# Keys of the second stage run one block further ahead of values

## The chip, the cores and the metric

The kernel runs on one core of a Trainium2 chip. The metric is the device time of one execution in microseconds (us), lower is better. A core has TensorE (PE, matmuls; its weight loads are listed as PEld), VectorE (DVE), ScalarE (ACT), GpSimd (POOL) and SyncE (SP, which here only starts DMAs). They run their own instruction lists in order and meet at semaphores.

## The reference, cut to what matters

```python
# layer 0: group norm, q/k/v, softmax attention over 4096 positions, output projection, residual
x = _L0_conv_ref(x, ...)
# layer 1
t = _to_tokens(x)                                   # (4, 4096, 128)
kv = silu(_ln_t(t) @ W_kv)                          # 8 heads x 128 keys and 8 x 128 values
s = einsum('hd,bthd->bth', q_proj, k)               # one score per head and token
m = cummax(s); e = exp(s - m); u = cumsum(e)
w = cumsum(e[..., None] * v); t = t + (w / u).mean(heads)
# top 2 of 8 experts by a softmax router, over the normed tokens
t = t + _L1_ffn_ref(_ln_t(t), router_w, router_b, expert_w, expert_b)
```

## The kernel before, in words

The first stage (layer 0) takes the first two thirds of the span and is not touched. The second stage (`scan_attention_and_experts`) does layer 1 for 32 blocks of 512 tokens: block i is chunk s = i // 4 of batch element i % 4. Four blocks with the same s are called a super here.

One loop over steps j = 0 to 43, with eight slots h in each, is written out on every engine. In slot h of step j an engine does its part for head h of the **values** of block j - 5 (V_LAG), for head h of the **keys** of block j, and for the **experts** of block j - 11 (F_LAG) or j - 12. So steps 0 to 4 have keys alone, 5 to 10 keys and values, 11 to 31 all three, 32 to 36 values and experts, the rest experts alone.

- Keys of a block: POOL makes xf (`scaled`, L1110) and xl (`low`, L1116), ACT rounds xh (`high`, L1333), PE runs three matmuls a head (`key`, L1242), ACT the silu (L1337), PE the scores of four heads at a time (`row_sums`, L1258). After the fourth block of a super its scores are complete, and VectorE turns them into weights in the next step (`rows_at`): running maximum and difference in slot 0 (L1441, L1447), after an exp on ACT in slot 2 (L1394, between two activation table loads) the running sum and a reciprocal in slot 3 (L1452, L1458), a product in slot 4 (L1462). SP writes these rows to DRAM (`weight_rows`, four DMAs) and reads them back spread over 128 partitions, half a block (1 MB) at a time (`weight_spread`, tile bq).
- The token norm of the super after the next also hangs on the key steps (`norm1_at`): ACT squares four blocks in slots 4 and 5, PE means in slot 6 and slot 0 of the next step, VectorE the variance (slot 1), ACT `norm_scale` in slot 7 of that step: Ln and Exp (L1326, L1328).
- Values of a head: PE three matmuls into one of three PSUM banks (`value`), which wait until the scan of head h - 3 is done; ACT silu (L1341) and one minus the weight (L1347); VectorE product (`weigh`, L1469) and scan along the tokens (`scan`, L1477). POOL adds the heads (L1131 to L1138), VectorE adds the residual (L1484).
- Experts: POOL gates four pairs (L1124, 1024 columns each), PE runs eight f32 matmuls (L1278), VectorE adds the result (`output`, L1496) at the start of slot 4. The router (`norm2_at`) works in steps j with j % 4 = 1 (logits on PE, `gate_scale` on ACT in slot 7: L1368, L1370) and 2 (choice of two experts on VectorE, slots 0 to 4). Where j % 4 = 1, `norm_scale` and `gate_scale` of the two norms stand between one pair of table loads (L1412, L1417).

The two norms and the router share one PSUM bank, st_ps.

By j % 4 the extra work before is: 0, rows and first half of the token norm; 1, its second half, logits, both scales, and the first use of the new weights; 2, choice of experts; 3, nothing. These are called here the steps of rows, of logits, of choice, and plain.

## Time and profile before

| | |
|---|---|
| time, median of 3 runs (lowest, highest) | 2654.93 us (2654.89, 2656.35) |
| the profiled execution: its own time | 2654.88 us |
| the profiled execution: span of the core | 2653.2 us |
| busy: PE, DVE, POOL, ACT | 95%, 83%, 77%, 70% |
| first value silu of step 5 | 1879.6 us |
| step 36, the last with values, begins | 2569.47 us |
| TensorE clock granted, mean | 0.99 |

Start times are microseconds from the beginning of the span. A step is read here from VectorE's product for head 0 (L1469) to the next step's. Busy times overlap between engines; an engine that is less busy than the stretch is long waited in it, and the profile names what ended its wait.

### The profile page before, as it was taken

What the parts mean: (1) busy time and instruction counts of PE and PEld (TensorE: products, weight loads), DVE (VectorE), ACT (ScalarE), POOL (GpSimd) and SP (SyncE); (2) the same over time, 40 slices, a digit from 0 to 9 for tenths busy, and PEclk for the clock granted to TensorE, in tenths of its full rate; (3) what the DMA queues carried; (4) which work ended last, traced back from release to release, by engine and by line L of the source; (5) the groups of instructions that cost most, each with busy time, mean ns of one, the idle gap of its engine ahead of it and who ended that gap; (6) DMA issues with size and microseconds to landing.
All of it is one profiled execution on the core that took longest, in us unless ns stands there. A gap on an engine that the chain in (4) does not pass through costs nothing.

```text
span 2653.2 us, 36314 instructions
## 1 busy us (share of the span) xinstructions
PE 2526.4 (95%) x10665; PEld 1836.3 (69%) x10665; DVE 2190.9 (83%) x3276; ACT 1855.0 (70%) x3414; POOL 2032.4 (77%) x1492
## 2 busy tenths in 40 slices
PE   6999999999999999999999999998889999999878
PEld 4788877788887778888778878875445555555443
DVE  6788887788888778888788888873699889988995
ACT  5677777677777767677776667776887777777650
POOL 5787877778887777887678877886458989888883
PEclk9999999999999999999999999999989999999999
DMA  1000000010000010000000100101435666565555
GB/s 68 5 13 9 9 13 9 10 43 9 9 17 9 9 41 9 13 13 9 9 9 9 37 13 9 40 21 49 155 134 214 227 228 237 185 257 209 208 211 215
DMA packets 58102, 198.35 MB, mean 75 GB/s; under 512 B 12752, under 2 KB 15376, under 8 KB 40496
## 3 DMA queue, kind: packets, MB, share of 16 engines
q1 hardware_dynamic: 57904, 196.03, 21.0%
q8 instruction: 85, 1.39, 0.2%
q14 instruction: 113, 0.93, 0.1%
HBM read 178.04 MB, written 17.96 MB: 74 GB/s over the span
## 4 chain that ended last, share of the span: by engine, by line
PE 46%; POOL 26%; issue 14%; DVE 7%; ACT 4%; DMA 2%; SPq 0%; POOLq 0%; DVEq 0%; ACTq 0%
POOL p_lo L222 23%; PE m_ps L360 5%; PE om_ps L389 5%; PE s_ps L375 5%; PE om_ps L391 5%; PE om_ps L390 5%; PE s_ps L377 5%; PE s_ps L376 5%; PE mo_ps L1278 3%; DVE v_ps L1469 2%; DVE ay L1477 2%; PE k_ps L1234 1%; PE row_ps L1258 1%; PE v_ps L1234 1%; DMA bq<-weight_rows 1%
## 5 line engine op out<-in xcount | busy, mean ns | idle before, releaser
L222 POOL TENSOR_TENSOR p_lo<-pf,p_hi 128x512 fp32r<-128x512 f32 x1024 | 1319.5, 1293 | 390.7 <-ACT p_hi L512 388.0
L507 ACT ACTIVATE pf<-s_ps 128x512 f32<-128x512 f32 x1024 | 613.2, 599 | 508.1 <-PE s_ps L377 506.8
L651 DVE TENSOR_REDUCE mx<-m_ps 128x1 f32<-128x512 f32 x1024 | 701.4, 686 | 255.1 <-PE m_ps L360 248.3
L667 DVE TENSOR_TENSOR sum_ps<-sum_ps,pf 128x512 f32<-128x512 f32 x960 | 662.1, 690 | 20.0 <-ACT pf L507 19.6
L512 ACT CAST p_hi<-pf 128x512 fp32r<-128x512 f32 x1024 | 627.3, 613 | 0.0
L375 PE MATMUL s_ps<-q_hi,kd_hi 128*128 128x512 f32 x1024 | 424.6, 415 | 0.0
L360 PE MATMUL m_ps<-w_both,q_hi 128*128 128x512 f32 x1024 | 404.8, 397 | 7.7 <-DVE mx L651 6.5
L389 PE MATMUL om_ps<-p_hi,v_hi 128*128 128x512 f32 x1024 | 401.8, 392 | 6.1 <-POOL p_lo L222 6.1
L377 PE MATMUL s_ps<-q_lo,kd_hi 128*128 128x512 f32 x1024 | 399.7, 390 | 0.0
L376 PE MATMUL s_ps<-q_hi,kd_lo 128*128 128x512 f32 x1024 | 399.7, 390 | 0.0
L390 PE MATMUL om_ps<-p_hi,v_lo 128*128 128x512 f32 x1024 | 399.1, 390 | 0.0
L391 PE MATMUL om_ps<-p_lo,v_hi 128*128 128x512 f32 x1024 | 398.9, 390 | 0.0
L1477 DVE TENSOR_TENSOR_SCAN ay<-ay,carry,v_ps 128x512 f32<-128x512 f32 x224 | 286.8, 1280 | 8.5
L1124 POOL TENSOR_TENSOR xg<-gate_b,tv 128x1024 f32<-128x1024 f32 x108 | 258.6, 2398 | 9.3 <-DMA gate_b<-gate_rows 3.6
L1278 PE MATMUL mo_ps<-xg,ew 128*128 128x512 f32 x464 | 234.9, 605 | 10.6 <-POOL xg L1124 9.3
L1341 ACT ACTIVATE v_ps<-v_ps 128x512 f32<-128x512 f32 x256 | 150.3, 587 | 131.1 <-PE v_ps L1236 129.4
L360 PEld LDWEIGHTS m_ps<-w_both,q_hi 128*128 128x128 f32 x1024 | 192.9, 188 | 62.6 <-DVE mx L651 19.5
L389 PEld LDWEIGHTS om_ps<-p_hi,v_hi 128*128 128x128 f32 x1024 | 192.1, 188 | 58.1 <-POOL p_lo L222 16.4
L375 PEld LDWEIGHTS s_ps<-q_hi,kd_hi 128*128 128x128 f32 x1024 | 192.6, 188 | 51.8 <-issue 15.1
L376 PEld LDWEIGHTS s_ps<-q_hi,kd_lo 128*128 128x128 f32 x1024 | 192.6, 188 | 49.9 <-issue 12.7
L377 PEld LDWEIGHTS s_ps<-q_lo,kd_hi 128*128 128x128 f32 x1024 | 192.3, 188 | 41.6
L391 PEld LDWEIGHTS om_ps<-p_lo,v_hi 128*128 128x128 f32 x1024 | 192.2, 188 | 40.5
(226 smaller groups left out, 3587.5 us busy)
## 6 DMA issues: line engine op xcount, KB each, us to landing
bq<-weight_rows SPq DMA_DIRECT2D x64, 1024.0 KB, 6.7
gate_b<-gate_rows SPq DMA_DIRECT2D x60, 1024.0 KB, 5.0
xb<-in_x_dram SPq DMA_DIRECT2D x8, 1024.0 KB, 6.1
rb_sb<-inverse_rows SPq DMA_DIRECT2D x32, 256.0 KB, 3.7
tokens<-xb SPq DMA_DIRECT2D x32, 256.0 KB, 2.0
tp<-tokens SPq DMA_DIRECT2D x32, 256.0 KB, 5.4
rb<-norm_rows SPq DMA_DIRECT2D x32, 256.0 KB, 5.5
tv<-tokens SPq DMA_DIRECT2D x32, 256.0 KB, 6.5
```

The lines of the kernel that those rows point to most:

```text
L222: nc.gpsimd.tensor_tensor(p_lo[:, r, :], pf[:, r, :], p_hi[:, r, :].bitcast(F32), ALU.subtract).then_inc(lo_done, 1)
L360: pe.matmul(m_ps[:, j % 2, :], q_hi[:, n % QRING, sub * C:(sub + 1) * C], kp[:, chunk * BANK:(chunk + 1) * BANK], start=True, stop=True).t ...
L375: pe.matmul(dst, kd_hi[:, ks], q_hi[:, q, :], start=False, stop=False, skip_group_check=True)
L376: pe.matmul(dst, kd_lo[:, ks], q_hi[:, q, :], start=False, stop=False, skip_group_check=True)
L377: pe.matmul(dst, kd_hi[:, ks], q_lo[:, q, :], start=False, stop=True, skip_group_check=True).then_inc(s_pe, 1)
L389: pe.matmul(o, v_hi[:, t, :], p_hi[:, r, :], start=(t == 0), stop=False)
L390: pe.matmul(o, v_lo[:, t, :], p_hi[:, r, :], start=False, stop=False)
L391: pe.matmul(o, v_hi[:, t, :], p_lo[:, r, :], start=False, stop=(t == KT - 1)).then_inc(pv_pe, 1)
L507: nc.scalar.activation(pf[:, g % RING, :], s_ps[:, g % 2, :], ACT.Exp, scale=SCALE).then_inc(exp_done, 1)
L512: nc.scalar.copy(p_hi[:, g % RING, :], pf[:, g % RING, :]).then_inc(hi_done, 1)
L651: nc.vector.tensor_reduce(mx[:, n % 2, sub, chunk:chunk + 1], m_ps[:, j % 2, :], AX.X, ALU.max).then_inc(m_max, 1)
L667: nc.vector.tensor_tensor(sum_ps[:], sum_ps[:], p, ALU.add).then_inc(sum_done, 1)
```

## The change

Keys no longer go with the step number alone. `key_slots(j, h)` gives the keys (block and head) that belong to slot h of step j: one head as a rule, two in the slots that AHEAD lists. In steps 5 to 8 that is slot 3, in steps 9 and 10 slots 2 and 5: eight heads, so one block. From step 11 on keys are those of block j + 1, and step 31 has none. Everything that hangs on the key steps moves with them, rows and token norm too; values, router and experts stay. `begun(j)` gives the blocks whose head 0 falls into step j, for SP's queue. The ring of xh and xl has eight places instead of seven. `norm_scale` gets its own pair of table loads. Room is made in SBUF: ebf and qcol lie in acc, rst2 in var2, place1 and place2 are one tile, zeros is one column that the scans read 512 times. `mean` waits for the gates of the super four back.

```diff
-    NP, NV, NX = 8, 9, 7
+    NP, NV, NX = 8, 9, 8
+    AHEAD = {V_LAG: (3,), V_LAG + 1: (3,), V_LAG + 2: (3,), V_LAG + 3: (3,), V_LAG + 4: (2, 5), V_LAG + 5: (2, 5)}
...
-        zeros = sb("zeros", [C, TOK])
+        zeros = sb("zeros", [C, 1])
...
+        def key_slots(j, h):
+            n = HEADS * j + h + sum(len(at) for step, at in AHEAD.items() if step < j) + sum(at < h for at in AHEAD.get(j, ()))
+            return [divmod(n + i, HEADS) for i in range(2 if h in AHEAD.get(j, ()) else 1)]
+
+        def begun(j):
+            return [k for h in range(HEADS) for k, e in key_slots(j, h) if e == 0]
...
+                for k in begun(j):
+                    if stage(k + NP):
+                        load_p(k + NP)
+                    if k % B == 2 and k // B + 1 < SUPERS:
+                        norm_rows(k // B + 1)
+                    if stage(k + 2) and k:
+                        spread(sp, k + 2)
...
-                if rows_at(j) is not None:
-                    weight_rows(rows_at(j))
+                for k in begun(j):
+                    if rows_at(k) is not None:
+                        weight_rows(rows_at(k))
...
             def mean(s):
+                after(pe, gt_act, s - 3)
...
-                    if stage(k):
-                        silu_key(k, h)
-                    if rows_at(j) is not None and h == 2:
+                    for k, e in key_slots(j, h):
+                        if stage(k):
+                            silu_key(k, e)
+                        if rows_at(k) is not None and e == 2:
...
+                        if norm1_at(k, 1) is not None and e == 7:
+                            nc.scalar.preload_act_table_set("natural_log_exp_and_others")
+                            norm_scale(norm1_at(k, 1))
+                            nc.scalar.preload_act_table_set("silu_and_others")
...
-                    if h == 7 and (norm1_at(j, 1) is not None or norm2_at(j, 1) is not None):
+                    if h == 7 and norm2_at(j, 1) is not None:
                         if norm2_at(j, 1) != SUPERS - 1:
                             nc.scalar.preload_act_table_set("natural_log_exp_and_others")
-                        if norm1_at(j, 1) is not None:
-                            norm_scale(norm1_at(j, 1))
-                        if norm2_at(j, 1) is not None:
-                            gate_scale(norm2_at(j, 1))
+                        gate_scale(norm2_at(j, 1))
                         nc.scalar.preload_act_table_set("silu_and_others")
...
-                    if rows_at(j) is not None:
-                        s = rows_at(j)
-                        if h == 0:
-                            maxima(s)
-                            shifted(s)
+                    for k, e in key_slots(j, h):
+                        if rows_at(k) is not None:
+                            s = rows_at(k)
+                            if e == 0:
+                                maxima(s)
+                                shifted(s)
```

POOL's `scaled` and `low`, PE's `key`, `row_sums`, `square_mean` and `mean`, ACT's `high`, squares and VectorE's `sums`, `inverse`, `new_weights` and `variance` are put under `key_slots` in the same way.

## Rows read from the trace of the kernel before

**Rows 1.** The page: busy time of the engines.
```profile
PE 2526.4 (95%) x10665; PEld 1836.3 (69%) x10665; DVE 2190.9 (83%) x3276; ACT 1855.0 (70%) x3414; POOL 2032.4 (77%) x1492
```

**Rows 2.** Engines by stretch: steps 20, 21, 22, 23 (rows, logits, choice, plain).
```profile
core 0: us, PE busy (x) PEld busy (x) DVE busy (x) ACT busy (x) POOL busy (x), PEclk, DMA share, GB/s
2205.16:2233.45 28.29, 26.47 (x112) 14.72 (x109) 25.38 (x24) 19.57 (x34) 25.74 (x15) 1.00 0.41 147
2233.45:2257.40 23.95, 23.95 (x107) 14.07 (x106) 19.45 (x22) 21.00 (x38) 21.40 (x13) 1.00 0.90 334
2257.40:2279.70 22.30, 20.54 (x80) 11.38 (x79) 21.50 (x39) 16.42 (x31) 17.47 (x12) 1.00 0.51 173
2279.70:2298.55 18.85, 18.85 (x78) 11.38 (x76) 17.89 (x20) 13.06 (x24) 18.85 (x12) 1.00 0.74 274
```

**Rows 3.** VectorE's waits, 1879 to 2590 us: total us, times, longest.
```profile
DVE v_ps L1469 <- DMA bq<-weight_rows: 17.1, 8, 6.8
```

**Rows 4.** Timeline of VectorE, steps 20 to 22: its waits, and slot 4's scan.
```profile
2215.79 0.70 DVE L1469 TENSOR_TENSOR v_ps<-bq,v_ps 128x512 f32<-128x512 f32 x1 [0.81 <-ACT v_ps L1341]
...
2224.11 1.28 DVE L1477 TENSOR_TENSOR_SCAN ay<-ay,carry,v_ps 128x512 f32<-128x512 f32 x1
...
2233.45 0.70 DVE L1469 TENSOR_TENSOR v_ps<-bq,v_ps 128x512 f32<-128x512 f32 x1 [1.75 <-DMA bq<-weight_rows]
...
2257.40 0.70 DVE L1469 TENSOR_TENSOR v_ps<-bq,v_ps 128x512 f32<-128x512 f32 x1 [4.07 <-ACT v_ps L1341]
```

**Rows 5.** Timeline of ScalarE at the end of step 21, slot 7.
```profile
2251.67 0.59 ACT L1337 ACTIVATE sk<-k_ps 128x512 f32<-128x512 f32 x1
2252.28 1.28 ACT L1412 ACT_TABLE_LOAD   x1
2253.57 0.72 ACT L1326 ACTIVATE v_r<-v_r,epsc 128x512 f32<-128x512 f32 x1
2254.33 0.63 ACT L1328 ACTIVATE v_r<-v_r 128x512 f32<-128x512 f32 x1
...
2256.72 0.58 ACT L1341 ACTIVATE v_ps<-v_ps 128x512 f32<-128x512 f32 x1
```

**Rows 6.** The chain of waits, step 23: pieces on TensorE (start, length).
```profile
2276.02 0.50 PE v_ps L1234
...
2276.97 1.00 PE row_ps L1258 x8
...
2281.11 0.86 PE mo_ps L1278 x2
...
2282.20 0.23 PE v_ps L1235
...
2297.13 0.23 PE v_ps L1234
```

**Rows 7.** Engines by stretch: steps 5, 9 and 11.
```profile
1884.55:1903.27 18.72, 14.79 (x64) 8.70 (x64) 15.89 (x18) 17.72 (x30) 8.45 (x6) 1.00 0.64 248
...
1957.71:1979.00 21.29, 18.08 (x91) 10.52 (x89) 17.23 (x21) 20.81 (x38) 13.63 (x11) 1.00 0.62 236
...
2000.70:2018.24 17.54, 15.45 (x67) 9.12 (x66) 17.26 (x18) 13.23 (x24) 14.83 (x10) 1.00 0.76 263
```

**Rows 8.** Timeline of VectorE, steps 8 to 10: weights done, and its waits.
```profile
1950.32 0.67 DVE L1462 TENSOR_TENSOR b_r<-b_r,e_r 128x512 f32<-128x512 f32 x1
...
1957.71 0.70 DVE L1469 TENSOR_TENSOR v_ps<-bq,v_ps 128x512 f32<-128x512 f32 x1 [1.18 <-DMA bq<-weight_rows]
```

**Rows 9.** The chain of waits, step 8: the DMAs of the weights.
```profile
1952.02 1.47 DMA weight_rows<-b_r
1953.50 4.19 DMA bq<-weight_rows
```

**Rows 10.** Engines by stretch: steps 31 (plain) and 32 (rows).
```profile
2465.30:2484.16 18.86, 18.86 (x78) 11.40 (x76) 17.91 (x19) 12.54 (x23) 18.51 (x11) 1.00 0.80 284
2484.16:2510.88 26.72, 20.22 (x57) 10.99 (x54) 24.94 (x24) 12.58 (x20) 20.31 (x12) 0.81 0.30 105
```

More of the change, by code:

```diff
@@ L873, in scan_attention_and_experts @@
         acc = sb("acc", [C, 2, TOK])
+        ebf, qcol = acc[:, 0, 0:C], acc[:, 1, 0:HEADS]
         carry = sb("carry", [C, B, HEADS])
@@ L879, in scan_attention_and_experts @@
         l_sb = sb("l_sb", [C, TOK])
-        var2, rst2 = sb("var2", [C, GRP]), sb("rst2", [C, GRP])
+        var2 = sb("var2", [C, GRP])
+        rst2 = var2
         msq2 = sb("msq2", [C, GRP])
-        top1, top2, place1, place2, share, gap = (sb(n, [C, GRP]) for n in ("top1", "top2", "place1", "place2", "share", "gap"))
+        top1, top2, foremost, share, gap = (sb(n, [C, GRP]) for n in ("top1", "top2", "foremost", "share", "gap"))
         pick1, pick2 = sb("pick1", [C, GRP, E]), sb("pick2", [C, GRP, E])
@@ L1069, in run_sync @@
                     load_v(v + 1)
-                if stage(k + NP):
-                    load_p(k + NP)
-                if j % B == 2 and j // B + 1 < SUPERS:
-                    norm_rows(j // B + 1)
-                if stage(k + 2) and k:
-                    spread(sp, k + 2)
+                for k in begun(j):
[5 more added lines that the diff above has]
+                        spread(sp, k + 2)
                 if j == 0:
@@ L1166, in run_gpsimd @@
             for j in range(STEPS + 1):
-                k, v = j, j - V_LAG
+                v = j - V_LAG
                 if j == 3:
@@ L1180, in run_gpsimd @@
                             pool.wait_ge(t2_dve, NBLK)
-                    if stage(k + 1) and h == 3:
-                        scaled(k + 1)
+                    for k, e in key_slots(j, h):
+                        if stage(k + 1) and e == 3:
+                            scaled(k + 1)
                     if stage(v) and h == 5:
@@ L1186, in run_gpsimd @@
                             carried(v, 0)
-                    if stage(k + 1) and h == 5:
-                        low(k + 1)
+                    for k, e in key_slots(j, h):
+                        if stage(k + 1) and e == 5:
+                            low(k + 1)
                     if stage(v) and h == 7:
@@ L1284, in run_tensor @@
                         value(v, h)
-                    if stage(k - 1) and h == 0:
-                        row_sums(k - 1, 1)
-                    if norm1_at(j, 1) is not None and h == 0:
-                        square_mean(norm1_at(j, 1))
-                    if stage(k):
-                        key(k, h)
-                    if stage(k) and h == 5:
-                        row_sums(k, 0)
-                    if norm1_at(j, 0) is not None and h == 6:
-                        mean(norm1_at(j, 0))
+                    for k, e in key_slots(j, h):
+                        if stage(k - 1) and e == 0:
+                            row_sums(k - 1, 1)
+                        if norm1_at(k, 1) is not None and e == 0:
+                            square_mean(norm1_at(k, 1))
+                        if stage(k):
+                            key(k, e)
+                        if stage(k) and e == 5:
+                            row_sums(k, 0)
+                        if norm1_at(k, 0) is not None and e == 6:
+                            mean(norm1_at(k, 0))
                     if norm2_at(j, 1) is not None and h == 5:
@@ L1440, in maxima @@
                 after(dve, d_dve, s)
-                nc.vector.tensor_tensor_scan(m_r[:], row_ps[:], zeros[:], LOWEST if s == 0 else m_r[:, TOK - 1:TOK],
+                nc.vector.tensor_tensor_scan(m_r[:], row_ps[:], zeros[:].to_broadcast([C, TOK]), LOWEST if s == 0 else m_r[:, TOK - 1:TOK],
                                              ALU.max, ALU.add).then_inc(m_dve, 1)
@@ L1451, in sums @@
                 after(dve, ri_dve, s)
-                nc.vector.tensor_tensor_scan(u_r[:], e_r[:], zeros[:], 0.0 if s == 0 else u_r[:, TOK - 1:TOK],
+                nc.vector.tensor_tensor_scan(u_r[:], e_r[:], zeros[:].to_broadcast([C, TOK]), 0.0 if s == 0 else u_r[:, TOK - 1:TOK],
                                              ALU.add, ALU.add).then_inc(u_dve, 1)
@@ L1596, in run_vector @@
                         scan(v, h)
-                    if rows_at(j) is not None:
-                        s = rows_at(j)
-                        if h == 0:
-                            maxima(s)
-                            shifted(s)
-                        if h == 3:
-                            sums(s)
-                            inverse(s)
-                        if h == 4:
-                            new_weights(s)
-                    if norm1_at(j, 1) is not None and h == 1:
-                        variance(norm1_at(j, 1))
+                    for k, e in key_slots(j, h):
+                        if rows_at(k) is not None:
+                            s = rows_at(k)
+                            if e == 0:
+                                maxima(s)
+                                shifted(s)
+                            if e == 3:
+                                sums(s)
+                                inverse(s)
+                            if e == 4:
+                                new_weights(s)
+                        if norm1_at(k, 1) is not None and e == 1:
+                            variance(norm1_at(k, 1))
                     if stage(v - 1) and h == 2:
```

37 lines of the change are left out of this document (18 added, 19 removed).

## The prediction

> **What bounds the kernel now.** I read the page first, then the engines step by step, then who waited, then the chain of waits. The page [rows 1] shows TensorE at 95% and VectorE at 83%, but a busy PE is counted with overlapping matmuls, and the mean hides that the steps differ. The stretches of one super [rows 2] are what counts: 28.29 us for the step of rows, 23.95 for logits, 22.30 for choice, 18.85 for the plain step, 93.4 together; steps 12 to 30 repeat this nearly to the tenth. VectorE is busy for 84.2 of the 93.4. In the steps of choice and plain it has hardly a gap, in the other two it has gaps of 3 and 4.5 us. So it is the bound in most slots, and the question is who holds it in the gaps.
>
> The waits [rows 3] name the spread weights, bq: 17.1 us over the stage in eight waits, one of them 6.8. The timeline [rows 4] gives the waits of a super their place, and shows that silus hold VectorE longer: 0.81 us behind the exp in the step of rows, 1.75 us for bq at the start of the step of logits, and 4.07 us at its end. Behind the last one stands a block on ScalarE [rows 5]: load, Ln, Exp, two small ones for the router, load, 4.45 us from 2252.28 to 2256.72 without a silu.
>
> TensorE has its own pace where nobody holds it. In the plain step [rows 6] a slot is six f32r matmuls of 0.23 and one f32 expert of 0.86 (two records): 2.25 us; row sums add 1.00 twice. From 2276.02 to 2297.13, less 0.27 for the slow first matmul, a plain step is 20.85 us of TensorE. VectorE needs 18.85 for it. It got away with 18.85 because in the step of choice TensorE had run ahead; there are three value banks, so the lead is at most two heads, and the plain step uses it up. So a super has two runs. In one VectorE sets the pace: choice, plain, and rows up to the scan of slot 4 (ends 2224.11 + 1.28 = 2225.39). There TensorE is let go for head 7, and from then on it and then ScalarE's block set the pace: 2257.40 - 2225.39 = 32.0 us to the next step of choice. This makes a check: slot 7 (2.25), a step (20.85), and square means, logits and transposes, some 3.0, less the last slot (2.25), are 23.85; then value matmuls and the start of the silu 1.0, one head on ScalarE 1.7, the block 4.45, a silu 0.7: 31.7 against 32.0. The wait for bq lies in the middle of this run, VectorE has slack there, and so it costs nothing of those 32.0. That is the main reading of this prediction.
>
> **What the change does, part by part.** The stage keeps its 44 steps, the first five and their wait for the first weights are as before, and the matmuls, silus, scans and DMAs are the same in number. Added are ten table loads on ScalarE (in five supers two norms had shared a pair). What changes is who is beside whom.
>
> (1) *Steps 5 to 9 take the extra heads.* A head of keys is 0.59 us of ScalarE [rows 5] and 0.7 of TensorE, which in these steps has no experts. In step 5 ScalarE is busy for 17.72 of 18.72 [rows 7]: one more silu, +0.5. In steps 6 and 7 one more per step hides behind VectorE. Step 9 is the dear one: ScalarE has 20.81 of 21.29. It gets two silus (1.2) and, as the norm's scale falls on slot 2 and the router's on slot 7, two more loads (2 x 1.28 = 2.6): 24.6, +3.3 on the path, since the slack it had is used before. Bounds: 0.5 if VectorE's lag covers it, 4.
>
> (2) *A wait is moved in SP's queue.* Rows of super 1 start in step 7, slot 5, and their product falls on step 8, slot 1. But `weight_rows(1)` stands in SP's list of step 7, ahead of the spread of the half block that step 8 needs in slot 4. SP sits there until the product. From the product's end (1950.99 in [rows 8]) the four issues take some 1.3 us and a spread 4.19 [rows 9], 5.5 to 6.7 us in all (the wait of before ended 6.7 after it). VectorE comes to slot 4 after two slots of 1.9 and a residual of 0.7, 4.5 us: it waits 1.0 to 2.2. The wait of 1.18 at the start of step 9 [rows 8] goes. Net 0 to +1, I take +0.5. In later supers the product is in slot 4 and the spread behind it is due a step later with 10 us to spare; load, store and gate spreads behind it have been released no earlier than that.
>
> (3) *Each later super.* Rows move into the plain step, so VectorE's run is now choice and rows; the plain work comes behind them, in TensorE's run, which has two steps. Per super: VectorE's plain step goes, -18.85; a plain step at TensorE's pace comes, +20.85; the 0.81 behind the exp goes, as VectorE still has lag from the step of choice; and the block ahead of the step of choice loses Ln and Exp of the token norm, 0.72 + 0.63 [rows 5], -1.35. Sum -0.16. The wait for bq goes and gives nothing back, by the reading above. The square means move one step within TensorE's run: nothing. Three supers, with rows in steps 15, 19 and 23: -0.5. In the fourth (rows in 27) no norm's scale is left to take out, so it would be +1.2; as TensorE's run is without its square means there, the wait for bq may have counted in part, so I take +0.6. Together +0.1, with -1 to +1 a super as bounds, since each of the prices may be off by 0.5.
>
> (4) *The norm's own block*, load, Ln, Exp, load, 3.9 us, now ends the step after rows. I cost it at nothing, since TensorE goes on beneath it. From its last key matmul it has the expert (0.86), slot 0 (3.4), slot 1 (2.25) and one value (0.7) that need no new silu, 7.2 us; ScalarE needs a silu (0.6), the block (3.9) and three activations of the next head (1.8), 6.3. The cover is 0.9 us. VectorE stalls 3 us there and catches up at 1.9 a slot against 2.25. Behind the block queue silus alone.
>
> Rows 5 show the load at 1.28 us and the Ln 1.29 us behind its start [rows 5]. The Trainium skill ("ScalarE: Activation LUTs", What ACT_TABLE_LOAD costs) counts a drain of 1.38 us to every switch, 2.66 in all. By it the ten new loads would be 26.6 us of ScalarE instead of 12.8, the cover in (4) would be short by some 1.9 us four times, step 9 longer by 2.8, and the sum about 10 us higher; the trace shows no such gap and I go by the row.
>
> (5) *The first super with experts.* Step 11 was 17.54 us at VectorE's pace [rows 7], not 18.85, so the same exchange is -17.54 + 20.85 - 1.35 = +2.0. The work on rows now runs where POOL has no gating, and may be cheaper. Bounds 0 and 2, I take +1.0.
>
> (6) *The end.* Step 31 has no keys but the last rows; TensorE is far from bound (eight heads of keys and the row sums, 7.6 us, gone). VectorE goes through 31 and 32 without gap. Of before go the gap that TensorE's pace left in step 31 (0.95) and the wait in step 32 (26.72 - 24.94 = 1.78) [rows 10]; busy times overlap a little, I take -1.9, between -1 and -2.7. That the last step of keys falls away is worth no more, though it is what the change buys with steps 5 to 10: step 31 was VectorE's to nearly the last slot. From step 34 on nothing differs.
>
> (7) `mean` waits for gates that are seven slots old; broadcast zeros, shared tiles and the ring of eight cost nothing (each xh waits for the same block of values, relative to its step, as before).
>
> Sum: (1) +3.8, (2) +0.5, (3) +0.1, (5) +1.0, (6) -1.9 = +3.5. The profiled execution took 2654.88 (1.7 us of it outside the span), the median is 2654.93, so they may be taken as one: **2658.4**.
>
> **Rivals.** *A: bq was the bound.* If VectorE is really what every slot waits for, the waits on bq [rows 3] except the first (17.1 - 6.8 = 10.3) come back in full, and the shorter block five times (6.8): with (1) and (2) 2654.9 - 10.3 - 6.8 + 4.3 = 2642. For it: the chain of waits passes through bq [rows 9]. Against: 24 us after the bq wait VectorE waits 4.07 again, for a silu [rows 4]. It decides if TensorE's two steps take less than about 20 us each. Chance 0.17.
>
> *B: the norm's block is not hidden.* One mechanism, in the slot after it, in steps 12, 16, 20 and 24: if TensorE comes to the block without its 0.9 of cover, it stalls, up to 3.9 us each, 15.6; at half, 8 us: 2666.4. It decides when a head on ScalarE takes half as long again as 1.8, or a wait on POOL's gating holds an expert in slots 0 and 1. Chance 0.2. The drain of 1.38 us a switch that the Trainium skill counts ("ScalarE: Activation LUTs", What ACT_TABLE_LOAD costs) would bring the same about; rows 5 have none.
>
> *C: the clock.* The granted clock is 0.81 of 2.4 GHz in step 32 [rows 10], a step of rows without keys, in which TensorE works for 20.2 of 26.7 us; it is 1.00 in step 20 [rows 2], where it has keys and experts. A mean of 0.81 over 26.72 us is 10.2 us at 1.2 GHz. Now choice and rows adjoin. Step 11 is likely to show it once, +2; in every super 1.7 each, 8.5 in all: 2667. Chance 0.08.
>
> **Numbers.** My forecast has 0.5, with 2653 to 2663 as its own range from the bounds of (1) to (6); 0.05 is for what I don't see. 0.2% is 5.3 us, about what a measurement of this kernel can tell from no change: faster is under 2649.6, slower over 2660.2. A quarter of my own case lies above. Slower 0.13 + 0.2 + 0.05, some of B and C being milder: 0.36. Faster 0.2 with A's share and the unseen. Same 0.44. The range reaches to the milder half of A and past B: 2646 to 2668.
>
> **What would show it.** Right: no wait for bq in steps 9, 13, 17 and on, but one in step 8, slot 4; supers of 93 us from choice to choice; from slot 4 of the step of rows to choice 51 to 52 us; step 9 some 3 us longer; ScalarE's block before choice 3.1 us. Wrong: supers of 91 or less (then A, the lead is longer than two heads), TensorE waiting on a key's silu in slot 1 or 2 behind the norm's block (B), a granted clock under 1 in steps 11 to 27 (C).

## The result, and the profile after

The changed kernel took 2661.6 us (median of 16 runs, one of them, 4212 us at a granted clock of 0.57, left out of the comparison), the kernel before 2655.2 beside it. The ratio is 1.0020, with a 95% interval of 1.0014 to 1.0027: some 5.3 us slower (the two medians are 6.4 apart), clear of no change and just at the 0.2% that was set as the border between "the same" and "slower". 2658.4 was predicted, in a range of 2646 to 2668.

The profiled execution of after took 2659.79 us, the one of before 2654.88. The account below is of this pair: +4.9. Its first view is the page:

```profile
PE 2531.9 (95%) x10665; PEld 1836.1 (69%) x10665; DVE 2179.0 (82%) x3276; ACT 1869.4 (70%) x3424; POOL 2036.4 (77%) x1492
```

Beside [rows 1] ScalarE has ten instructions more, the ten table loads, and 14.4 us more. TensorE has 5.5 us more, POOL 4.0 more and VectorE 11.9 us less, each with as many instructions as before; where VectorE's 11.9 went is seen under terms (3) and (5). The page does not say where 5 us of the span went. The steps do. This table gives the length of each group of steps, from VectorE's first product in it to that of the next group, as the windows and the timeline have it, and beside it what the prediction's terms add up to:

| steps | before, us | after, us | change | predicted |
|---|---|---|---|---|
| up to 5 | 1884.55 | 1885.84 | +1.3 | 0 |
| 5 to 9 | 94.45 | 103.23 | +8.8 | +4.3 (terms 1, 2) |
| 10 to 13 | 91.62 | 90.53 | -1.1 | +1.0 (term 5) |
| 14 to 25, three supers | 280.16 | 276.45 | -3.7 | -0.5 (term 3) |
| 26 to 29 | 92.23 | 92.36 | +0.1 | +0.6 (term 3) |
| 30 to 33 | 86.52 | 87.41 | +0.9 | -1.9 (term 6) |
| 34 and 35 | 39.94 | 39.94 | 0 | 0 |
| rest | 83.7 | 82.3 | -1.4 | 0 |
| span | 2653.2 | 2658.1 | +4.9 | +3.5 |

The first line and the one called rest are noise: the code there does the same work, and in the twelve profiles of this case step 5 starts anywhere between 1884.6 and 1886.6, and what lies behind the start of step 36 is anywhere between some 81 and 84. In between every group but one is off its term by two to four and a half microseconds, with both signs. So the sum was good and the terms were not, and the experiments go after the three large ones: steps 5 to 9, the supers, steps 30 to 33.

One profile is one execution. In four profiles with the code of after in steps 5 to 9 (after and experiments 3, 4 and 6) these steps took 103.2, 103.8, 104.2 and 105.0 us; in three with the code of before (before, (c) of experiment 5 and experiment 7) 94.5, 94.9 and 95.2. The loss there is thus 8.0 to 10.6 us, and a difference of under 2 us in these steps between two profiles says little. The supers repeat within 0.1 us.

The engines by stretch in after, steps 7, 8 and 9, then rows, logits and choice of a later super (19 is the step of rows, 20 the plain one, 21 logits, 22 choice), then 31, 32 and 33:

```profile
1920.19:1939.72 19.53, 16.75 (x74) 10.42 (x73) 17.23 (x20) 17.19 (x30) 12.90 (x9) 1.00 0.25 90
1939.72:1963.48 23.76, 18.83 (x84) 9.27 (x88) 21.80 (x23) 18.80 (x36) 11.81 (x9) 0.93 0.46 171
1963.48:1989.07 25.59, 21.59 (x101) 11.61 (x97) 17.14 (x21) 22.86 (x39) 14.17 (x10) 0.93 0.46 159
...
2194.04:2218.54 24.50, 22.68 (x98) 12.38 (x97) 24.15 (x24) 19.08 (x32) 21.95 (x13) 1.00 0.54 193
2218.54:2241.73 23.19, 23.19 (x92) 14.14 (x91) 18.57 (x21) 17.58 (x29) 23.19 (x14) 1.00 0.85 324
2241.73:2263.90 22.17, 22.17 (x100) 12.80 (x99) 16.97 (x21) 19.48 (x36) 21.18 (x13) 1.00 0.70 251
2263.90:2286.18 22.28, 21.52 (x85) 12.32 (x84) 21.48 (x38) 16.53 (x31) 17.73 (x12) 1.00 0.46 151
...
2470.70:2495.82 25.12, 18.42 (x45) 9.26 (x43) 24.77 (x25) 13.53 (x21) 18.72 (x11) 0.80 0.46 172
2495.82:2513.48 17.66, 14.95 (x43) 7.12 (x42) 17.38 (x20) 9.59 (x17) 17.66 (x11) 1.00 0.78 290
2513.48:2535.82 22.34, 19.01 (x68) 9.80 (x67) 18.64 (x21) 14.22 (x25) 21.54 (x11) 0.92 0.81 294
```

In a super the reader should see what [rows 2] showed of before, in another order: VectorE with hardly a gap in choice and rows (busy for 21.48 of 22.28 and 24.15 of 24.50), TensorE without a gap in the two steps behind them (23.19 and 22.17, both fully busy). The plain step, 18.85 at VectorE's pace before, is 23.19 now. A super is 92.15 us against 93.4.

VectorE's waits over the same stretch as [rows 3], by group, first the silus' of before, then both of after:

```profile
DVE v_ps L1469 <- ACT v_ps L1341: 36.4, 26, 4.1
...
DVE v_ps L1485 <- ACT v_ps L1355: 60.6, 44, 3.7
DVE v_ps L1485 <- DMA bq<-weight_rows: 8.3, 2, 6.8
```

The eight waits for bq are two, 6.8 at the first weights as before and one of 1.5. 8.8 us of waiting for transfers are gone, the waits for silus have grown by 24.2, from 26 to 44 of them, and the kernel is not faster.

### The profile page after: what moved, and what is told of

Read it like the earlier page. It is cut to its first block, busy times and chain, and to the rows that moved or that the text cites. A ratio compares the mean times of both kernels' runs of the same rounds, so it can differ in the third digit from the quotient of the medians.

```text
span 2658.1 us, 36327 instructions
## 1 busy us (share of the span) xinstructions
PE 2531.9 (95%) x10665; PEld 1836.1 (69%) x10665; DVE 2179.0 (82%) x3276; ACT 1869.4 (70%) x3424; POOL 2036.4 (77%) x1492
## 4 chain that ended last, share of the span: by engine, by line
PE 48%; POOL 26%; issue 14%; DVE 6%; ACT 5%; DMA 1%; SPq 0%; POOLq 0%; DVEq 0%; ACTq 0%
POOL p_lo L222 23%; PE m_ps L360 5%; PE om_ps L389 5%; PE s_ps L375 5%; PE om_ps L391 5%; PE om_ps L390 5%; PE s_ps L377 5%; PE s_ps L376 5%; PE mo_ps L1291 4%; DVE ay L1493 2%; DVE v_ps L1485 2%; PE k_ps L1247 1%; PE row_ps L1271 1%; PE v_ps L1247 1%; PE k_ps L1249 1%
## 5 line engine op out<-in xcount | busy, mean ns | idle before, releaser
L1291 PE MATMUL mo_ps<-xg,ew 128*128 128x512 f32 x464 | 238.0, 612 | 15.4 <-POOL xg L1134 14.4
L1485 DVE TENSOR_TENSOR v_ps<-bq,v_ps 128x512 f32<-128x512 f32 x256 | 174.6, 682 | 69.2 <-ACT v_ps L1355 60.6
```

## The experiments

Each run gives its median against runs of the kernel before on the same chip. "After" is the changed kernel. Sums are from the start of step 5 of the profiled execution: to step 10 it is 94.45 in before and 103.23 in after, to step 36 it is 684.92 and 689.92.

**1. Was the wait for bq free?** In the kernel before, the first half of the weights of each super is taken from the rows of the super before it, which are long there: other data, no wait.

```diff
             def weight_spread(i, j):
                 s, b, cols = place(i)
+                s -= s > 0 and b == 0 and j == 0
...
-                if stage(v + 1) and j % B != 0:
+                if stage(v + 1) and (j % B != 0 or j > V_LAG):
                     weight_spread(v + 1, 0)
...
-                if stage(v + 1) and j % B == 0:
+                if stage(v + 1) and j % B == 0 and j < V_LAG:
                     weight_spread(v + 1, 0)
```

> The kernel before, with the first half block of weights of each super taken from the rows of the super before it (wrong weights for four heads of 7 blocks), so that its spread is issued ahead of the rows and VectorE's and ScalarE's wait for bq in steps 9, 13, 17, 21, 25, 29 and 33 is gone; nothing else is moved. Theory of the prediction (that wait lies in the run in which TensorE sets the pace and costs nothing): from step 5 to step 36 684.9 less 0 to 3 us, with what there is in steps 28 to 33, where TensorE has less to do, and supers still 93.4 less at most 0.3. Rival A (VectorE is the bound and each wait counts): 10 us less, supers of 91.6.

2656.6 against 2656.3: 1.0001 (0.9991 to 1.0010), and 684.89 to step 36. VectorE's waits in it have no row for bq behind the first weights; what they have instead is longer waits for silus. The engines in its steps 20 and 21:

```profile
2207.13:2233.61 26.48, 24.64 (x106) 13.55 (x103) 25.33 (x23) 20.19 (x34) 23.92 (x14) 1.00 0.47 166
2233.61:2259.41 25.80, 25.80 (x114) 15.24 (x112) 18.96 (x23) 20.55 (x37) 24.76 (x16) 1.00 0.88 334
```

26.48 + 25.80 = 52.28, where [rows 2] have 28.29 + 23.95 = 52.24. Step 20 is 1.8 us shorter, the whole wait, and step 21 is 1.85 longer: TensorE, busy for all of its 25.80 us, comes when it comes. This refutes rival A on the kernel before itself, and shows the main reading. It is not so in every step. Steps 28 and 29 together are 1.0 shorter (50.1 for 51.1), as term (3) had allowed for the fourth super; steps 12 and 13 are 0.8 longer and step 35 is 0.7 longer, for which the traces give no reason. The sum of all is nothing.

**2. Is the block ahead of choice on the path?** In the kernel before, one more pair of loads between its two scales (steps 9, 13, 17, 21, 25).

```diff
                         if norm1_at(j, 1) is not None:
                             norm_scale(norm1_at(j, 1))
+                        if norm1_at(j, 1) is not None and norm2_at(j, 1) is not None:
+                            nc.scalar.preload_act_table_set("silu_and_others")
+                            nc.scalar.preload_act_table_set("natural_log_exp_and_others")
```

> The kernel before, with a second pair of table loads (2 x 1.28 = 2.57 us) between the two norms' scales at the end of steps 9, 13, 17, 21, 25; nothing else. It measures what a microsecond of ScalarE's block just ahead of the step of choice costs. Theory of the prediction (this block is wholly on the path, so taking Ln and Exp, 1.35 us, out of it was worth 1.35 a super): supers of 93.4 + 2.6 = 96.0, step 5 to step 36 684.9 + 12.9 = 697.8. Rival (TensorE runs ahead under the block and gives part back in the step of choice): 1.0 to 2.0 a super, 690 to 695. By the Trainium skill's drain of 1.38 us for each switch ('ScalarE: Activation LUTs', What ACT_TABLE_LOAD costs) the pair would be 5.3 us, 711.

2669.9, 1.0054 (1.0037 to 1.0071); to step 36 699.35, 14.4 more, and the supers are 2.7 us longer each. ScalarE's timeline at the end of its step 21:

```profile
2263.93 0.63 ACT L1328 ACTIVATE v_r<-v_r 128x512 f32<-128x512 f32 x1
2264.58 1.28 ACT L1416 ACT_TABLE_LOAD   x1
2265.87 1.28 ACT L1417 ACT_TABLE_LOAD   x1
2267.17 0.31 ACT L1368 ACTIVATE rst<-var,epsc 128x16 f32<-128x16 f32 x1
```

Two loads are 2.59 us from the first one's start to the next activation's, and the kernel pays 2.7 to 2.9 for them: the block is on the path in full, and the 1.35 that the change took out of it was rightly counted. The Trainium skill ("ScalarE: Activation LUTs", What ACT_TABLE_LOAD costs) counts 2.66 us for each switch, a load of 1.28 and a drain of 1.38, which would be an estimate of 5.3 for the pair here and of 26.6 for the ten loads of the change. The trace agrees on the load and shows no drain: a load is 1.28 us here and the next instruction starts 1.29 to 1.30 behind its start.

**3. Is the norm's own block hidden, and by how much?** In after, the same pair of loads in that block, in steps 12, 16, 20 and 24.

```diff
                             nc.scalar.preload_act_table_set("natural_log_exp_and_others")
+                            if j > V_LAG + 6:
+                                nc.scalar.preload_act_table_set("silu_and_others")
+                                nc.scalar.preload_act_table_set("natural_log_exp_and_others")
                             norm_scale(norm1_at(k, 1))
```

> The changed kernel, with a second pair of table loads (2.57 us) in the token norm's own block at the end of steps 12, 16, 20 and 24, where the prediction costed the block at nothing. Theory (TensorE has 7.2 us of work under a need of 6.3, so 0.9 of the 2.57 is covered): 1.7 us a super, 6.7 in four; from step 5 to 36 689.9 + 6.7 = 696.6. Rival B (the block is not hidden at all): 2.57 each, 10.3, 700.2. Rival (well hidden, since POOL and not TensorE sets the pace in the steps behind rows, POOL being busy for 23.19 of 23.19 us in step 20): under 1 us in all.

2676.5, 1.0077 (1.0062 to 1.0092); to step 36 706.82, 16.9 us more than after. 2.6 of that lies in steps 5 to 11, which the edit does not reach, so it belongs to this execution; behind them the four blocks cost 14.4 (the medians of this run and of after are 14.9 apart). That is over what either theory expected (6.7 and 10.3). TensorE's timeline behind the block of step 20:

```profile
2255.83 0.50 PE L1247 MATMUL k_ps<-xh,w_both 128*128 128x512 f32 x1 [2.12 <-ACT sk L1351]
```

This is the key of slot 2, where the prediction had put the stall. Of 2.57 us added 2.12 come through, so the cover was 0.45, not 0.9. In after itself no such wait is in the stretch of steps 20 and 21: it has TensorE busy throughout. The block is hidden there, with half a microsecond in hand. The other part of the cost is seen in the engines of the step with the stall, in two of the supers of this run (17 and 21):

```profile
2158.64:2182.26 23.62, 22.56 (x95) 13.06 (x96) 16.84 (x21) 19.55 (x36) 18.11 (x10) 0.93 0.58 204
...
2254.77:2276.76 21.99, 20.93 (x95) 12.16 (x96) 18.42 (x21) 19.45 (x36) 17.60 (x10) 1.00 0.55 188
```

The same work, with 1.63 us between them, and a granted clock of 0.93 in one. By block, steps 12 and 13 and then the three supers were longer by 4.0, 4.0, 2.35 and 4.0, the cheap one being that with the clock at 1.00 behind its gap. So a gap of 2.12 us in a full TensorE cost 2.35 us where the clock stayed, and 1.65 more in the three places where it did not. I had not thought of the second when I gave both expectations.

**4. Does POOL's gating set the pace of TensorE's two steps?** In after, POOL gates only the first of each pair of blocks 8 to 12 (half the work, so the output is another). One execution.

```diff
+                n = 1 if 8 <= f <= 12 else 2
+                nc.gpsimd.tensor_tensor(xg[:, p % 2, 0:n, :], gate_pair(f, p)[:, 0:n, :], twice(tv[:, f % NV, :])[:, 0:n, :],
...
```

> The changed kernel, with POOL gating only the first of each pair of experts in blocks 8 to 12 (steps 19 to 23), so that POOL has some 5 us less work a step and gets out of VectorE's way; the second expert of each pair reads stale data. It tells who sets the pace from slot 4 of the step of rows to the step of choice, 51.6 us in the changed kernel, where TensorE and POOL are both busy throughout step 20 (23.19 of 23.19). Theory of the prediction (TensorE's pace and ScalarE's block): that run stays within 0.5 us of 51.6. Rival (POOL's pace): it falls by 2 us or more. And the other run, choice and rows up to slot 4's scan (40.6 us in the changed kernel, 2 us less than the sum of its parts before, of which 0.8 is the wait behind the exp): if VectorE's residual and running sum are slower beside POOL's work, it falls by another 1 us or more; if not, it stays.

2658.35. TensorE's run, from slot 4 of rows in step 19 to the choice of step 22, first in after, then in this run:

```profile
2212.31:2263.90 51.59, 51.54 (x220) 30.07 (x221) 41.66 (x48) 40.45 (x70) 48.05 (x28) 1.00 0.76 273
```

```profile
2212.50:2264.09 51.59, 51.53 (x220) 30.07 (x221) 41.60 (x49) 40.41 (x70) 38.88 (x29) 1.00 0.75 273
```

51.59 both times, with 9 us of POOL less. TensorE sets the pace there, and 51 to 52 was predicted. VectorE's run before it, choice and rows up to slot 4's scan, went from 40.56 to 40.29. In the next super, where the gating is halved from the run's start, it is 40.00, and the two instructions that are shorter there are

```profile
2293.32 1.29 POOL L1135 TENSOR_TENSOR xg<-gate_b,tv 128x512 f32<-128x512 f32 x1 [0.54 <-issue]
...
2294.00 1.16 DVE L1502 SCALAR_TENSOR_TENSOR tv<-acc,tv 128x512 f32<-128x512 f32 x1
2297.00 1.26 DVE L1470 TENSOR_TENSOR_SCAN u_r<-e_r,u_r,zeros 128x512 f32<-128x512 f32 x1
```

where after has 1.47 and 1.50. POOL's gating does lengthen them; terms (3) and (5) below come back to it.

**5. What made steps 5 to 9 cost 8.8 us?** Four ways of placing things anew in after. First, SP's queue: the spread for slot 4 goes ahead of the weights' issue.

```diff
+                if stage(v + 1) and j % B != 0 and j > V_LAG:
+                    weight_spread(v + 1, 1)
                 for k in begun(j):
                     if rows_at(k) is not None:
                         weight_rows(rows_at(k))
...
-                if stage(v + 1):
+                if stage(v + 1) and (j % B == 0 or j <= V_LAG):
                     weight_spread(v + 1, 1)
```

> The changed kernel, with the issue of the weight rows put behind the spread of the second half block in SP's list of the steps that are no multiple of four (steps 7, 11, 15 and on). Measured best from VectorE's product for head 0 in step 5 to that in step 36: 684.92 us before, 689.92 changed. Theory (the moved wait in SP's queue costs its 1.52 us in step 8, slot 4, and nothing in other steps): that wait is gone, step 8 shrinks by up to 1.5 us, but step 9, where ScalarE and TensorE are behind, gives back what lag was lost, so the stretch is 0.5 to 1.5 us shorter, 688.4 to 689.4, and steps 11 to 30 are the same to the tenth. Rival (the wait lay under something else, or the queue order matters in every super): 689.9, or several us less with all supers shorter.

2658.3, 1.0011 (1.0002 to 1.0020). Step 8 is 22.29 for 23.76, all of the wait of 1.52, and step 9 stays (25.72). But at step 13 the two kernels are level again (171.55 and 171.59); the 1.7 us that this profile is ahead at step 36 (688.24) come from steps 28 and 32 to 33. The last slots of step 11, where TensorE's run begins, in after and in this run:

```profile
2027.45:2034.25 6.80, 6.20 (x31) 3.13 (x32) 6.69 (x9) 3.39 (x6) 4.25 (x3) 1.00 0.54 190
```

```profile
2027.00:2033.64 6.64, 6.64 (x28) 3.09 (x28) 6.53 (x7) 3.39 (x6) 4.09 (x3) 0.74 0.54 175
```

TensorE got 0.74 of its clock here and the next step was 24.02 instead of 23.19. Whether the edit brought that or this execution did isn't settled; step 12 is 23.2 in the other profiles with after's code. The median is lower than after's, but the intervals of the two ratios overlap.

Then the places of the eight extra heads. (a) Four each in steps 5 and 6. (b) None in step 9, four in step 10.

```diff
-    AHEAD = {V_LAG: (3,), V_LAG + 1: (3,), V_LAG + 2: (3,), V_LAG + 3: (3,), V_LAG + 4: (2, 5), V_LAG + 5: (2, 5)}
+    AHEAD = {V_LAG: (1, 3, 5, 7), V_LAG + 1: (1, 3, 5, 7)}
```

```diff
+    AHEAD = {V_LAG: (3,), V_LAG + 1: (3,), V_LAG + 2: (3,), V_LAG + 3: (3,), V_LAG + 5: (0, 2, 4, 6)}
```

> The changed kernel, with the eight extra heads of keys in slots 1, 3, 5, 7 of steps 5 and 6 instead of over steps 5 to 10, so that the order of the later supers holds from step 7: norm scale at the end of step 8, away from the router's work in step 9. Theory (the start costs 8.8 us over before mainly because step 9 has two extra heads and two extra pairs of loads' work on ScalarE within one step, all with VectorE idle): steps 5 and 6 get longer by 1 to 3 us together (four silus of 0.59 each on ScalarE in steps where it has 1 us of room), step 9 falls from 25.6 to 22 to 23, and from step 5 to step 10 the stretch of 103.2 us falls by 3 to 5 us; later steps are as in the changed kernel. Rival (any place for the block's keys costs the same, since the work of ScalarE and TensorE is what is dear): the stretch from step 5 to 10 stays within 1 us of 103.2.

> The changed kernel, with the two extra heads of step 9 given to step 10 (slots 0, 2, 4, 6), where VectorE has the router's choice to do and a lag of 4 to 5 us. Theory (two more heads in step 9 are on the path at what ScalarE and TensorE need for them): step 9 shrinks from 25.6 by 1.2 (two silus) to 2.8 us (two heads on TensorE too), step 10 stays at 21.7, and the stretch from 5 to 36 is 687.1 to 688.7. Rival (step 9 is long only from the norm's block on ScalarE, 3.9 us at slot 2 or 3): step 9 at 25 or more, the stretch within 0.5 us of 689.9.

(a) 2658.9, 1.0009 (1.0000 to 1.0019), and 101.04 to step 10, 2.2 better than after, where 3 to 5 was expected: steps 5 and 6 are 3.9 us longer than before and not 1 to 3. (b) 2659.9, 1.0014 (1.0005 to 1.0024), and 102.52, 0.7 better, which is within what the same code differs by from profile to profile. Step 9 was 25.59 in after; in (a) and in (b) it is

```profile
1967.26:1987.60 20.34, 17.85 (x84) 10.96 (x84) 16.15 (x20) 19.46 (x36) 11.70 (x10) 0.92 0.43 156
```

```profile
1963.35:1987.95 24.60, 18.88 (x92) 9.95 (x91) 16.22 (x21) 21.43 (x36) 13.52 (x10) 0.93 0.43 153
```

Step 9 is 25.6 in all four profiles with after's code, so its 24.60 in (b) is clear: the two silus that step 9 had been charged with are worth 1.0 of its 4.3. In (a) the rows fall wholly into step 7, which becomes 23.80, the norm's block stands at the end of step 8, and step 9 is shorter than in before, but 6.6 us in all stay. What both keep is the norm's separate block and the rows brought forward; that these make up the rest is argued from the waits shown below, not shown by a run of its own.

(c) All eight heads in step 10. Then the rows run in step 8 as in before, both scales fall on one slot and share one pair of loads, and nothing of steps 5 to 9 changes.

```diff
+    AHEAD = {V_LAG + 5: tuple(range(8))}
...
-                            nc.scalar.preload_act_table_set("silu_and_others")
+                            if not (norm2_at(j, 1) is not None and h == 7):
+                                nc.scalar.preload_act_table_set("silu_and_others")
...
-                        if norm2_at(j, 1) != SUPERS - 1:
+                        if norm2_at(j, 1) != SUPERS - 1 and not any(norm1_at(k, 1) is not None and e == 7 for k, e in key_slots(j, h)):
```

> The changed kernel, with all eight extra heads in step 10, one in each slot, and the two norms' scales again between one pair of loads where both fall on the same slot (step 9 only). Steps 5 to 9 are then those of the kernel before. Theory (the dear part of the change is that the extra heads and the norm's own block fall on steps 5 to 9, where ScalarE and TensorE hold VectorE; in step 10 VectorE has the router's choice to do and the others have room: TensorE 13 us of work in 21.7): step 5 to 10 94.5 us instead of 103.2, step 10 22 to 24 us instead of 21.7, later steps as in the changed kernel, so the stretch to step 36 is 689.9 - 8.8 + 0.3 to 2.3 = 681.4 to 683.4, 1.5 to 3.5 under before. Rival (the extra block costs its 7.6 us of TensorE wherever it is put): step 10 at 27 or more, 686 to 690.

2655.0, 0.9995 (0.9986 to 1.0004). 94.93 to step 10, and step 10, which takes eight heads, is 23.24 for 21.70:

```profile
1980.03:2003.27 23.24, 22.01 (x100) 13.89 (x101) 21.09 (x38) 19.75 (x39) 10.96 (x9) 0.93 0.23 87
```

It stands 6.3 us ahead of after at step 12. To step 36 it is 684.03, somewhat above the 681.4 to 683.4 expected. Steps 5 to 9 were the loss of this change; steps 31 to 33 of this run are 65.15 us, as in after.

**6. Steps 31 to 33.** In after, POOL gates half of blocks 20, 21 and 22 (the output is another).

```diff
+                n = 1 if f in (20, 21, 22) else 2
...
```

> The changed kernel, with POOL gating only the first of each pair of experts in blocks 20, 21 and 22 (512 columns instead of 1024; the second keeps stale data), which fall on steps 31 to 34. Theory (the end of the stage gained nothing because POOL, busy from 2494.5 to 2530.9 without a gap, is the bound in steps 32 and 33 once rows and keys are gone from them): step 33 falls from 22.3 to about 18.7, steps 31 to 33 together from 65.1 to 61 to 62, from step 5 to 36 686 to 687. Rival (TensorE at its lower clock in step 33, granted 0.92, did it): steps 31 to 33 stay above 63.5.

2654.8, 0.9997 (0.9988 to 1.0006), and steps 31 to 33 are 24.04 + 16.96 + 18.24 = 59.24 where after has 65.12, 5.9 us less (61 to 62 was expected). Its step 33:

```profile
2513.05:2531.29 18.24, 17.39 (x67) 8.95 (x67) 17.04 (x22) 14.23 (x25) 14.18 (x10) 1.00 0.82 297
```

In after TensorE's waits in steps 32 and 33 name POOL, and POOL has no gap from 2492.17 until its own 0.80 ahead of 2531.72. By group, after:

```profile
PE mo_ps L1291 <- POOL xg L1134: 5.4, 3, 2.6
```

So POOL held step 33, which gives 4.1 of the 5.9. Steps 31 and 32 stay VectorE's (23.69 busy of 24.04 and 16.68 of 16.96); they are 1.1 and 0.7 shorter because VectorE's residual is, 1.23 and 1.19 us for 2.32 and 1.90. Some of step 33 is clock: with the gating whole it is 20.15 in run (b), at a granted clock of 1.00:

```profile
2512.02:2532.17 20.15, 17.76 (x68) 9.12 (x67) 17.74 (x21) 14.21 (x25) 20.15 (x11) 1.00 0.81 289
```

That is not 2.2 us gained, though: in (b) the low clock fell into step 32 (0.91), which is 18.54 for 17.66. The two steps together are 38.69 against 40.00, so the place of the low clock is worth at most 1.3 here, and POOL the rest.

**7. A version better than both.** (c), and two of the late pairs gated by VectorE instead of POOL.

```diff
-            return f >= LAST or (f >= FREE and f % 2 == 1 and p % 2 == 1)
+            return f >= LAST or (f >= FREE and f % 2 == 1 and p % 2 == 1) or (f, p) in ((21, 3), (22, 1))
...
```

> The version with all extra heads in step 10 and joined table loads, and two of POOL's gatings moved to VectorE (the fourth pair of block 21 and the second of block 22, both in step 33); same results. In the former run steps 31 to 33 took 65.2 us with POOL busy throughout, against 59.3 with half of the gating left out. Theory (POOL is the bound there, VectorE has gaps of 3 us in step 33): POOL's list shrinks by 4.8 us and VectorE's grows by 2 x 1.3: step 33 falls from 22.4 to 19.5 to 20.5, from step 5 to 36 684.0 falls to 681.5 to 682.5, 2.4 to 3.4 us less than before the change (684.9), ratio about 0.999. Rival (VectorE has no room, its added 2.6 us are on the path): 683.5 to 686.

2653.1 (11 runs) against 2655.9: 0.9989 (0.9980 to 0.9998), and 682.59 to step 36. Step 33 gives only 1 us (21.43, 19.5 to 20.5 was expected): with two gatings of 1.2 us added, VectorE is busy for 20.45 of it and now holds the step itself. It is the one version here that is faster than before, by 0.1%, and only just clear of no change.

## Why the prediction came out as it did

**The main reading held.** The waits on bq cost nothing (experiment 1), and a super is two runs, one of VectorE and one of TensorE (experiment 4). From slot 4 of rows to choice 51.5 was predicted by 32.0 + 20.85 - 1.35, and 51.59 is measured. The block before choice is 3.16 us (3.1 predicted) and lies on the path. VectorE's timeline in after shows what stands at its two ends:

```profile
2241.73 0.70 DVE L1485 TENSOR_TENSOR v_ps<-bq,v_ps 128x512 f32<-128x512 f32 x1 [3.69 <-ACT v_ps L1355]
2263.90 0.69 DVE L1485 TENSOR_TENSOR v_ps<-bq,v_ps 128x512 f32<-128x512 f32 x1 [2.87 <-ACT v_ps L1355]
```

VectorE waits 3.7 us behind the norm's block at the end of step 20 and catches up within the run; it waits 2.87 behind the router's block, for 4.07 in [rows 4]. Term (4), nothing, was right; its margin was half what I gave it. Experiment 3 says that rival B was nearer than it looked: half a microsecond more in the block and TensorE stalls, with the clock's price on top.

**Term (1) was mis-sized: 3.8 predicted.** With (2) it was 4.3 and 8.8 is measured. Here is VectorE in steps 7 to 9 of after:

```profile
1939.72 0.70 DVE L1485 TENSOR_TENSOR v_ps<-bq,v_ps 128x512 f32<-128x512 f32 x1 [1.61 <-ACT v_ps L1355]
...
1954.65 0.70 DVE L1485 TENSOR_TENSOR v_ps<-bq,v_ps 128x512 f32<-128x512 f32 x1 [1.52 <-DMA bq<-weight_rows]
...
1972.23 0.69 DVE L1485 TENSOR_TENSOR v_ps<-bq,v_ps 128x512 f32<-128x512 f32 x1 [1.54 <-ACT v_ps L1355]
...
1981.99 0.70 DVE L1485 TENSOR_TENSOR v_ps<-bq,v_ps 128x512 f32<-128x512 f32 x1 [2.46 <-ACT v_ps L1355]
...
1989.07 0.70 DVE L1485 TENSOR_TENSOR v_ps<-bq,v_ps 128x512 f32<-128x512 f32 x1 [2.86 <-ACT v_ps L1355]
```

The step of the prediction that failed is "in steps 6 and 7 one more per step hides behind VectorE" and with it the reading that step 9 alone is dear. By step, 5 to 9 changed by +0.1, +0.1, +4.2, +0.1 and +4.3, where +0.5, 0, 0, +0.5 and +3.3 stood in the prediction. The rows that begin in step 7 bring their 1.95 us on VectorE from step 8 and ScalarE's block for the exp, of 3.2 us. VectorE has half of that in hand there and waits 1.61 for the silu behind it, just ahead of the first product of step 8, so within step 7. Step 8 gives the 1.95 away, takes 1.35 of the norm's variance from step 9, and has the new wait of 1.52 where the old one of 1.18 stood at its end: 23.76 for 23.69. Step 9 should have become shorter by that 1.35. It is 4.3 longer: ScalarE is busy for 22.86 of 25.59 us, with two blocks that hold up silus, and VectorE's waits of 1.54, 2.46 and 2.86 stand one behind the other, with two of 0.63 between them. Over the five steps VectorE's waits for silus went from 6.1 us to 12.5. I had added new work to the step's old length, and not asked whether the old length was still that of the same work. Run (c), which leaves all of it out, is 8.3 lower than after at step 10 and pays 1.5 in step 10 and 0.4 in step 11.

**Term (2) was right in mechanism.** The new wait is at step 8, slot 4, and 1.52 long (1.0 to 2.2 predicted). Experiment 5 takes it away and step 8 becomes 1.47 shorter. The old one of 1.18 at the end of step 8 is gone, so the exchange is +0.34 for the +0.5 that I took.

**Terms (3) and (5) were too high, by 1.1 a super and by 2.1.** TensorE's run came out to a tenth; the difference is in VectorE's. It went from 61.36 us to 40.56, where 18.85 + 0.81 less would be 41.7. The residual and the running sum that fall into the step of rows were 2.16 and 1.82 us in before and are in after

```profile
2201.67 1.46 DVE L1500 SCALAR_TENSOR_TENSOR tv<-acc,tv 128x512 f32<-128x512 f32 x1
...
2204.97 1.50 DVE L1468 TENSOR_TENSOR_SCAN u_r<-e_r,u_r,zeros 128x512 f32<-128x512 f32 x1
```

That is 1.0 of the 1.1. They are quicker since they meet another operation of POOL. The residual takes 0.67 us where POOL leaves it alone. Here is what is under way on POOL when it starts, in before (residual from 2212.81 to 2214.97) and in after (2201.67 to 2203.13):

```profile
2212.05 2.38 POOL L1124 TENSOR_TENSOR xg<-gate_b,tv 128x1024 f32<-128x1024 f32 x1
```

```profile
2201.30 1.28 POOL L1120 TENSOR_TENSOR xf<-tp,rb 128x512 f32<-128x512 f32 x1
```

In both it ends 0.55 us behind POOL's operation, and so it does with the halved gating in experiment 4 (2294.00 to 2295.16, POOL until 2294.61). That holds throughout the timelines of before, after and experiments 4 and 6: a residual that starts while POOL is at work ends 0.54 to 0.56 us behind the end of that operation, a running sum 1.07 to 1.09 behind it, and alone they take 0.67 and 1.26. So each of the two waits out the operation that it meets, and the change moved the residual from a gating to a shorter rescaling of keys.

Term (5) is the same, and larger. I took 1 us off for rows without gating beside them. The two instructions in before (step 12), then in after (step 11):

```profile
2025.88 2.32 DVE L1484 SCALAR_TENSOR_TENSOR tv<-acc,tv 128x512 f32<-128x512 f32 x1
...
2030.03 2.73 DVE L1452 TENSOR_TENSOR_SCAN u_r<-e_r,u_r,zeros 128x512 f32<-128x512 f32 x1
```

```profile
2018.40 0.67 DVE L1500 SCALAR_TENSOR_TENSOR tv<-acc,tv 128x512 f32<-128x512 f32 x1
...
2020.90 1.26 DVE L1468 TENSOR_TENSOR_SCAN u_r<-e_r,u_r,zeros 128x512 f32<-128x512 f32 x1
```

That is 3.1 us less, and +2.0 less 3.1 is the -1.1 that steps 10 to 13 show. Over the whole second stage the 32 residuals and seven running sums take 13.9 us less in after, which covers the 11.9 by which VectorE's busy time fell.

**Term (6) had the wrong sign: -1.9 predicted, +0.9 measured.** VectorE's gaps did go: steps 31 and 32 are 25.12 + 17.66 = 42.78 for 45.58. But I costed the end as VectorE's alone. POOL has some 18.6 us of work to a step there (18.51 in step 31 of [rows 10]), more than the 17.66 that VectorE needs where no keys are made. Before, the step of rows stood between the plain steps and let POOL catch up; now 32 and 33 adjoin, POOL's debt falls due in 33, and that step is 22.34 for 18.65, +3.7, of which the clock has at most 1.3 (experiment 6).

**Rival C** came about in a mild form. The granted clock is 0.92 or 0.93 in steps 8 to 11, where the rival expected it in step 11, 0.92 in step 33, and 0.76 in the last 6.23 us before step 28; in steps 12 to 26, where it had put its price, it is 1.00 throughout. It is no reason for the loss in steps 5 to 9. Before had 1.00 in step 9 [rows 7], but 0.86 in step 8:

```profile
1934.02:1957.71 23.69, 19.10 (x82) 11.16 (x81) 22.18 (x23) 18.47 (x31) 13.12 (x9) 0.86 0.16 61
```

At half speed for the rest, 0.86 over step 8 is at most 3.3 us, and 0.93 over both steps 8 and 9 of after at most 3.5. And in the profile of experiment 4 step 8, with the same code, is 23.89 at 1.00, for 23.76 at 0.93. Step 28 is 19.96 where run (b) had 18.87, so 1.1 us of this profile's end belong to its execution. Against the terms, steps 5 to 9 are off by +4.5 and the end by +2.8, the first super by -2.1, the later ones by -3.2 and -0.5: +7.3 and -5.8, which leaves 1.5. That the total came near was luck in that part: the sum had the main reading right, and two misses that cancelled, the start and the end too cheap, VectorE's residuals and running sums too dear.

## What to carry to other kernels

A removed wait is worth what the next engine in line leaves of it: before counting it as a gain, look whether a longer wait for another engine follows within the same run, and in doubt feed the waiter old data and measure, which is one edit. Where engines take turns in setting the pace, a step moved from one's run to the other's changes its price (18.85 became 20.85 at TensorE's pace); cost each move at the pace of the run that it lands in, and cost every engine there, the one that is usually in the background too, and look what it has under way where an instruction lands: the same residual took from 0.67 to 2.75 us. The start of a stage, where no lag has been built up, and its end, where debts fall due, need their own account: they made 9.7 us of loss here against 3.7 of gain in twelve steps of the steady part.

## What was not expected of the hardware

A residual or running sum on VectorE that starts while POOL works on something waits that operation out: the residual takes 0.67 us alone, 2.16 where a gating of 2.38 was under way and 1.46 where a rescaling of 1.28 was, and ends 0.55 us behind POOL's operation in each case. The products for the heads and the running maximum, which have a tile in PSUM among their operands (v_ps, row_ps), show nothing of it beside the same work: 0.67 to 0.70 and 1.26 us throughout.

A gap of 2.12 us in an otherwise full TensorE was followed in three of four places by a step at a granted clock under 1 (0.93 in step 17, 23.62 us for 21.99): the gap's price nearly doubled. And the same instructions in different executions found the low clock in different places: steps 32 and 33 had 1.00 and 0.92 in one profile (17.66 and 22.34 us), 0.91 and 1.00 in another (18.54 and 20.15). A single step can differ by 2.2 us that way while the pair differs by 1.3, so compare stretches and not steps there.
